# The squares of the even heads' rectified scores move from GpSimd to ScalarE, in a fused attention and mixture-of-experts kernel

## The chip, the cores and the metric

The kernel runs on one core of a Trainium2 chip. The metric is the device time of one execution in microseconds; runs of one kernel are compared by their medians. The profile is one further execution, taken by the hardware profiler.

## The reference

Sixteen batches of 256 tokens of width 128 pass through an attention layer with 16 heads (keys of 16, values of 64) and an expert layer (16 experts and a shared one). What matters here is the attention's non-linearity, which is no softmax:

```python
sim = jnp.einsum('bhid,bhjd->bhij', queries, keys)
attn = jnp.square(jax.nn.relu(sim))
aggr = jnp.einsum('bhij,bhjd->bhid', attn, values)
out = tanh_norm(aggr) * jnp.tanh(jax.nn.silu(gates))
```

Around it stand a layer norm, the projections of queries, keys, values and gates, the l2 norms of the heads, the output projection with its residual, a second layer norm, a router (group selection, top 4 of 16), the gate, up and down products of all experts, and a second residual.

## The kernel before

The kernel is a software pipeline written out by hand. A **step** s handles one batch in each of its stages at once: the layer norm and the query and key projections of batch s+2 ("L"), values and gates of batch s+1 ("P"), attention of batch s ("A"), output projection and second norm of batch s-1 ("O"), experts of batch s-2 ("F"). Steps run from -2 to 17, so attention is present in steps 0 to 15. Each step has eight **slots** k; in slot k attention handles the pair of heads 2k and 2k+1, and TensorE also does a list of other jobs, named in the table `FILL`. Every engine has its own program in the order of these slots, and semaphores tie them together.

In slot k TensorE does the fillers of the slot (L369 to L371 are the three-part products of the projections and experts, L422 a transpose, L428 a spread of per-row scales, L432 and L451 the output and down products, L437 the transpose of the second norm's rows), then the scores of the NEXT pair (`scores`, L478, into `ps_s`), then the products of THIS pair's squares with the values (L507, into `ps_a`). So between a pair's scores and their use lie the fillers of one slot.

ScalarE in slot k rectifies the pair's scores, one instruction for each head (L607, `ps_s` to `r`), squares the odd head (L610, `r` to `p`), then squares the previous pair's result for its norm (L619, `big<-ps_a`, called a2), then empties the slot's filler banks: queries and keys (L560, L562), values and their squares (L567, L570), gates (L576, and their tanh at L545), expert gates (L599), transposes (L586, L590, L591). GpSimd squares the even head in the same slot (L338, `r` times `r`), and has besides only two tiny roots a step (L330) and four scalings of the values (L354, slots 4 to 7). VectorE gates each pair's result (L904), sums the squares of the values (L748), takes the head norms by Newton steps (L662 to L670), runs the router (L800 to L843, ending in the expert weights `cs`, L794), and empties other banks (L741, L859, L867, L876, L883).

The filler banks are four, used in turn: a job may start when the job four places before it in the list has been read. This is how a late reader on ScalarE or VectorE holds up TensorE.

Of the kernel before, what the change touches and what calls it, by code (L numbers as in the profile page):

```python
# [8 lines left out]
ALU = mybir.AluOpType  # L9
# [12 lines left out]
def bass_attn_moe_layer_kernel(nc, tokens, Wqg, Wkv, Wout, gate_kernel, gate_bias,  # L22
# [45 lines left out]
    with ExitStack() as ctx:  # L68
# [3 lines left out]
        def sem(name):  # L72
            return ctx.enter_context(nc.semaphore(name))
# [101 lines left out]
        done = {k: sem(f"{k}_done") for k in JOBS}  # L175
        read = {k: sem(f"{k}_read") for k in JOBS}
        scores_done, values_done = sem("scores_done"), sem("values_done")
        relu_done, probs_even, probs_odd = sem("relu_done"), sem("probs_even"), sem("probs_odd")
        a2_done, aw_done = sem("a2_done"), sem("aw_done")
        ln1_ready, xh_ready, rstd1_ready, rstd2_ready = sem("ln1_ready"), sem("xh_ready"), sem("rstd1_ready"), sem("rstd2_ready")  # L180
        qk_squared = sem("qk_squared")
# [113 lines left out]
        @block.gpsimd  # L295
        def _(pool):
            n = [0]

            def built(ins):
                n[0] += 1  # L300
                ins.then_inc(consts_pool, 1)
                pool.wait_ge(consts_pool, n[0])


            built(pool.memset(minus_half[:], -0.5))
            built(pool.memset(ident[:], 0.0))
            built(pool.affine_select(out=ident[:], in_=ident[:], compare_op=ALU.not_equal, fill=1.0, base=0,
                                     pattern=[[-1, P]], channel_multiplier=1))
            built(pool.memset(selraw, 0.0))
            for part in range(2):  # L310
                view = selraw.rearrange("k c (e m) -> k c e m", e=2)
                built(pool.affine_select(out=view, in_=view, compare_op=ALU.not_equal, fill=1.0, base=-H * part,
                                         pattern=[[-2, NP], [-1, 2], [0, DV]], channel_multiplier=1))

            built(pool.memset(pick[:], 0.0))
            view = pick[:, 0:H].rearrange("p (a j e) -> p a j e", j=4, e=2)
            built(pool.affine_select(out=view, in_=view, compare_op=ALU.not_equal, fill=1.0, base=0,
                                     pattern=[[-2, 2], [-32, 4], [-1, 2]], channel_multiplier=1))
            view = pick[:, H:3 * H].rearrange("p (c j) -> p c j", j=8)
            built(pool.affine_select(out=view, in_=view, compare_op=ALU.not_equal, fill=1.0, base=-8,  # L320
                                     pattern=[[-32, 4], [-1, 8]], channel_multiplier=1))

            built(pool.memset(head16[:], 1.0))
            built(pool.affine_select(out=head16[:], in_=head16[:], compare_op=ALU.is_ge, fill=0.0, base=8 * DK,
                                     pattern=[[-DK, 32]], channel_multiplier=1))
            built(pool.affine_select(out=head16[:], in_=head16[:], compare_op=ALU.is_ge, fill=0.0, base=DK - 1 - 8 * DK,
                                     pattern=[[DK, 32]], channel_multiplier=-1))

            def root(dst, src, ready):
                pool.tensor_tensor(dst[:], src[:], minus_half[:].broadcast_to([P, T]), ALU.pow).then_inc(ready, 1)  # L330

            def step(s, q, on, at):
                for k in range(SLOTS):
                    if "A" in on:
                        h = 2 * k
                        wait(pool, values_done, 8 * s + k - 1)
                        pool.wait_ge(relu_done, 16 * s + h + 1)
                        pool.tensor_tensor(p[h % 4][:], r[0][:], r[0][:], ALU.mult).then_inc(probs_even, 1)  # L338
                    if k == 1 and "L" in on:
                        pool.wait_ge(ch_l, 3 * (s + 3))  # L340
                        root(rstd1, var1, rstd1_ready)
                    if k == 6 and "O" in on:
                        pool.wait_ge(ch_n, 3 * s)
                        root(rstd2, var2, rstd2_ready)
                    if "P" in on:
                        b = s + 1
                        if k in (4, 5, 6, 7):

                            t, half = divmod(k - 4, 2)
                            pool.wait_ge(vs_ready, b + 1)  # L350
                            pool.wait_ge(read["v"], 4 * b + k - 3)
                            view = v[1 - q][:, t, half * 512:(half + 1) * 512].rearrange("p (h d) -> p h d", d=DV)
                            scale = vs[:, t, half * NP:(half + 1) * NP]
                            pool.tensor_tensor(view, view, broadcast(scale, [P, NP, DV], 2), ALU.mult)\  # L354
                                .then_inc(v_normed, 1)

            run_steps(pool, step)


        @block.tensor  # L360
        def _(pe):
# [122 lines left out]
            def step(s, q, on, at):  # L484
                n = 0
                for k in range(SLOTS):
                    for stage, kind, j in FILL[k]:
                        if stage in on:
                            wait_for_bank(n, s, at)
                            filler(stage, kind, j, s, q, on, at)  # L490
                        n += 1

                    if k < SLOTS - 1:
                        if "A" in on:
                            scores(s, q, k + 1)
                    elif at is None or "A" in stages(at + 1):
                        scores(s + 1, 1 - q, 0)
                    if "A" in on:
                        wait(pe, aw_done, 8 * s + k - 1)
                        if k == 0:  # L500
                            pe.wait_ge(v_normed, 4 * s + 4)
                        for t in range(T):
                            for e in range(2):
                                h = 2 * k + e
                                if t == 0:
                                    pe.wait_ge((probs_even, probs_odd)[e], 8 * s + k + 1)
                                last = pe.matmul(ps_a[k % 2][64 * e:64 * e + 64, 0:N],  # L507
                                                 v[q][:, t, h * DV:(h + 1) * DV], p[h % 4][:, t * N:(t + 1) * N],
                                                 start=(t == 0), stop=(t == T - 1))
                        last.then_inc(values_done, 1)  # L510
# [5 lines left out]
        def _(act):  # L516
# [84 lines left out]
            def step(s, q, on, at):  # L601
                for k in range(SLOTS):
                    if "A" in on:
                        for h in (2 * k, 2 * k + 1):
                            wait(act, (probs_even, probs_odd)[h % 2], 8 * s + k)
                            act.wait_ge(scores_done, 16 * s + h + 1)
                            act.activation(r[h % 2][:], ps_s[h % 2][:], ACT.Relu).then_inc(relu_done, 1)  # L607
                        wait(act, values_done, 8 * s + k - 1)
                        act.wait_ge(relu_done, 16 * s + h + 1)
                        act.activation(p[h % 4][:], r[1][:], ACT.Square).then_inc(probs_odd, 1)  # L610

                    if ("A" in on and k > 0) or ("O" in on and k == 0):
                        pair, b = (k - 1, s) if k > 0 else (NP - 1, s - 1)
                        if pair == 0:
                            wait(act, done["ones"], s + 2)
                            if at == 0:
                                act.wait_ge(w_lo, 4)
                        act.wait_ge(values_done, 8 * b + pair + 1)
                        act.activation(a2[:, pair, :], ps_a[pair % 2][:, 0:N], ACT.Square).then_inc(a2_done, 1)  # L619
                    for stage, kind, j in FILL[k]:  # L620
                        if stage in on:
                            evacuate(stage, kind, j, s, q)
                        if (kind, j) == ("gu", 4) and "O" in on:
                            act.wait_ge(n_ready, s)
                            act.activation(nn[:], nn[:], ACT.Tanh).then_inc(tanh_n, 1)
                    for stage, kind, j in FILL[k - 1] if k > 0 else ():
                        if kind == "g" and stage in on and at != -1:
                            gates(j, s, q)
                    if at == 0 and k == 5:
                        expert_weights()  # L630
                if at == -1:

                    for j in range(4):
                        gates(j, s, q)
# [408 lines left out]
```

## Time and profile before

| what | us |
|---|---|
| median of 3 runs (797.83 to 801.03) | 798.34 |
| the profiled execution | 800.48 |
| its span, first to last instruction | 798.7 |
| busy: TensorE matmul | 686.5 (86%) |
| busy: TensorE weight loads (beside the matmuls) | 541.4 (68%) |
| busy: ScalarE | 502.6 (63%) |
| busy: VectorE | 485.6 (61%) |
| busy: GpSimd | 225.2 (28%) |

By the page's chain of the work that ended last, TensorE holds 53% of the span, VectorE 21%, ScalarE 12%. TensorE was granted 0.936 of its full clock on average. A busy share is an average over stretches that are bound by different engines, so it doesn't say by itself what an added instruction costs; for that the chain and the idle times have to be read place by place.

### The profile page before, as it was taken

Reading aid. Unit: us, or ns where it says so; the run is one execution under the profiler, and the core shown is the slowest. Engines: PE = TensorE matmul, PEld = TensorE weight load, DVE = VectorE, ACT = ScalarE, POOL = GpSimd, SP = SyncE. Lnnn points to the kernel's source line nnn. Section 1 sums busy time; section 2 is a strip of 40 time slices with the busy share of each in tenths; the row PEclk is TensorE's granted clock in tenths of the full one; section 3 lists DMA queues with packets and bytes.
Section 4 is the critical chain, followed back from the end, with each engine's and each line's share of the span. In section 5 each row is a group of like instructions: output and inputs, shape, how many; then the busy total and the mean of one; then the engine's idle time right before and its main releaser. Section 6 shows DMA issues by size and latency. Waiting matters only on the chain.

```text
span 798.7 us, 16206 instructions
## 1 busy us (share of the span) xinstructions
PE 686.5 (86%) x5160; PEld 541.4 (68%) x5160; DVE 485.6 (61%) x1739; ACT 502.6 (63%) x1114; POOL 225.2 (28%) x240
## 2 busy tenths in 40 slices
PE   1576798989989898999989898998989899989785
PEld 1454576858767686867767686876768686767675
DVE  3545657576565748576575757556584756655653
ACT  2387786676857666775766667585766667564311
POOL 2224331423223231422323242322323141331000
PEclk9878999999989999998999999899999899998898
DMA  8894869191734819093572909175471909200000
GB/s 201 133 149 54 127 99 108 25 143 25 130 50 83 91 60 118 7 137 41 99 78 70 101 31 133 21 118 60 88 83 53 118 0 139 35 14 2 7 8 7
DMA packets 72801, 60.83 MB, mean 76 GB/s; under 512 B 8624, under 2 KB 72496, under 8 KB 72752
## 3 DMA queue, kind: packets, MB, share of 16 engines
q1 hardware_dynamic: 72752, 60.26, 51.4%
q8 instruction: 21, 0.34, 0.2%
q14 instruction: 28, 0.23, 0.1%
HBM read 41.37 MB, written 18.87 MB: 75 GB/s over the span
## 4 chain that ended last, share of the span: by engine, by line
PE 53%; DVE 21%; ACT 12%; issue 8%; DMA 2%; POOL 1%; SPq 1%; ACTq 0%; DVEq 0%; POOLq 0%
PE ps_a L507 8%; PE ps_f L432 7%; PE ps_f L369 7%; PE ps_f L451 5%; PE ps_f L370 5%; PE ps_f L371 5%; PE ps_f L428 5%; PE ps_s L478 4%; ACT r L607 3%; PE ps_f L411 2%; DVE norms_m L748 2%; ACT sq L570 2%; DVE it L859 2%; DMA qkt<-qk_rows 2%; PE ps_f L422 2%
## 5 line engine op out<-in xcount | busy, mean ns | idle before, releaser
L338 POOL TENSOR_TENSOR p<-r 128x512 f32<-128x512 f32 x128 | 134.2, 1049 | 486.7 <-ACT r L607 484.4
L607 ACT ACTIVATE r<-ps_s 128x512 f32<-128x512 f32 x256 | 138.8, 598 | 66.1 <-PE ps_s L478 65.8
L507 PE MATMUL ps_a<-p,v 128*64 128x256 f32 x1024 | 139.5, 393 | 2.3 <-DVE big L904 1.3
L904 DVE TENSOR_TENSOR big<-ps_a,wt 128x256 f32<-128x256 f32 x128 | 53.8, 421 | 103.6 <-ACT big L619 103.6
L507 PEld LDWEIGHTS ps_a<-p,v 128*64 128x64 f32 x1024 | 62.8, 137 | 38.7 <-issue 2.9
L610 ACT ACTIVATE p<-r 128x512 f32<-128x512 f32 x128 | 80.9, 632 | 11.6
L859 DVE TENSOR_TENSOR it<-ps_f,it 128x256 f32<-128x256 f32 x144 | 59.0, 419 | 38.1 <-ACT it L599 37.0
L599 ACT ACTIVATE it<-ps_f 128x256 f32<-128x256 f32 x144 | 54.2, 391 | 34.1 <-PE ps_f L371 33.6
L451 PE MATMUL ps_f<-wdown,it 128*128 128x128 f32 x576 | 71.3, 280 | 2.9 <-DVE it L876 1.7
L451 PEld LDWEIGHTS ps_f<-wdown,it 128*128 128x128 f32 x576 | 68.5, 196 | 4.5 <-DVE it L876 1.8
L354 POOL TENSOR_TENSOR v<-v,vs 128x512 f32<-128x512 f32 x64 | 66.7, 1045 | 10.5 <-DVE vs L782 10.4
L478 PE MATMUL ps_s<-qkt 64*128 64x256 f32 x512 | 66.4, 337 | 2.7 <-DMA qkt<-qk_rows 2.6
L876 DVE TENSOR_TENSOR it<-ps_f,it 128x512 f32<-128x512 f32 x64 | 44.0, 689 | 37.8 <-PE ps_f L428 37.2
L432 PE MATMUL ps_f<-wout,big 128*128 128x128 f32 x512 | 62.4, 275 | 0.8 <-DVE big L867 0.8
L432 PEld LDWEIGHTS ps_f<-wout,big 128*128 128x128 f32 x512 | 59.7, 192 | 1.2 <-DVE big L867 1.2
L748 DVE TENSOR_REDUCE norms_m<-sq 128x8 f32<-128x512 f32 x64 | 43.7, 684 | 27.2 <-ACT sq L570 26.6
L422 PE MATMUL ps_f<-ident,cs 128*32 128x128 f32 x32 | 8.2, 351 | 58.6 <-DVE cs L794 58.6
L478 PEld LDWEIGHTS ps_s<-qkt 64*128 64x128 f32 x512 | 39.7, 191 | 25.3 <-issue 10.6
L576 ACT ACTIVATE wt<-ps_f 128x512 f32<-128x512 f32 x64 | 38.4, 601 | 27.6 <-PE ps_f L371 27.1
L619 ACT ACTIVATE big<-ps_a 128x256 f32<-128x256 f32 x128 | 47.1, 368 | 8.9 <-PE ps_f L411 8.6
L369 PE MATMUL ps_f<-x2h,weg_hi 128*128 128x256 f32 x144 | 49.7, 345 | 2.2 <-ACT sq L570 0.5
L867 DVE TENSOR_TENSOR big<-ps_f,big 128x512 f32<-128x512 f32 x64 | 41.0, 683 | 16.5 <-PE ps_f L428 16.4
(154 smaller groups left out, 1563.2 us busy)
## 6 DMA issues: line engine op xcount, KB each, us to landing
qk_rows<-qk_parts SPq DMA_DIRECT2D x16, 1024.0 KB, 4.4
qkt<-qk_rows SPq DMA_DIRECT2D x64, 256.0 KB, 9.5
qkt<-qk_rows SPq DMA_DIRECT2D x128, 128.0 KB, 9.0
x_in<-in_L_attn_tokens SPq DMA_DIRECT2D x16, 128.0 KB, 2.1
x_res<-in_L_attn_tokens SPq DMA_DIRECT2D x16, 128.0 KB, 14.2
out<-o_sb SPq DMA_DIRECT2D x16, 128.0 KB, 14.2
big<-in_L_attn_Wqg SPq DMA_DIRECT2D x1, 640.0 KB, 4.3
big<-in_L_attn_Wkv SPq DMA_DIRECT2D x1, 640.0 KB, 5.5
```

Of the source, the lines that this page charges most:

```text
L338: pool.tensor_tensor(p[h % 4][:], r[0][:], r[0][:], ALU.mult).then_inc(probs_even, 1)
L354: pool.tensor_tensor(view, view, broadcast(scale, [P, NP, DV], 2), ALU.mult)\
L369: pe.matmul(dst, stat[0], mov[0], start=True, stop=False)
L432: last = pe.matmul(ps[:, 0:D], aw[pb][:, c, tok[j]], wout[:, c, :], start=(c == 0), stop=(c == NP - 1))
L451: last = pe.matmul(ps[:, 0:D], it[:, c, tok[j]], wdown[:, c, :], start=(c == 0), stop=(c == FC - 1))
L478: last = pe.matmul(ps_s[e][:, t * N:(t + 1) * N], qkt[q][rows, 1, k, t * P:(t + 1) * P], qkt[q][rows, 0, k, :], start=True, stop=True)
L507: last = pe.matmul(ps_a[k % 2][64 * e:64 * e + 64, 0:N], v[q][:, t, h * DV:(h + 1) * DV], p[h % 4][:, t * N:(t + 1) * N], start=(t == 0), ...
L599: act.activation(it[:, j, :], ps[:, 0:N], ACT.Silu).then_inc(silu_done, 1)
L607: act.activation(r[h % 2][:], ps_s[h % 2][:], ACT.Relu).then_inc(relu_done, 1)
L610: act.activation(p[h % 4][:], r[1][:], ACT.Square).then_inc(probs_odd, 1)
L748: dve.tensor_reduce(ssv[:, t, half * NP:(half + 1) * NP], squares_at(j).rearrange("p (h d) -> p h d", d=DV), AX.X, ALU.add)\
L859: dve.tensor_tensor(it[:, c, :], bank[("gu", c)][:, N:2 * N], it[:, c, :], ALU.mult)\
```

## The change

GpSimd no longer squares the even heads. ScalarE does it: after the two rectifications of a pair come two squares, even head first. One semaphore (`probs_done`) now counts the squares of both heads, where two counted before. Nothing else is altered; buffers and their sizes stay.

```diff
@@ GpSimd
                 for k in range(SLOTS):
-                    if "A" in on:
-                        h = 2 * k
-                        wait(pool, values_done, 8 * s + k - 1)
-                        pool.wait_ge(relu_done, 16 * s + h + 1)
-                        pool.tensor_tensor(p[h % 4][:], r[0][:], r[0][:], ALU.mult).then_inc(probs_even, 1)
                     if k == 1 and "L" in on:
@@ TensorE
                                 if t == 0:
-                                    pe.wait_ge((probs_even, probs_odd)[e], 8 * s + k + 1)
+                                    pe.wait_ge(probs_done, 16 * s + h + 1)
@@ ScalarE
                         for h in (2 * k, 2 * k + 1):
-                            wait(act, (probs_even, probs_odd)[h % 2], 8 * s + k)
+                            wait(act, probs_done, 16 * s + h - 1)
                             act.wait_ge(scores_done, 16 * s + h + 1)
                             act.activation(r[h % 2][:], ps_s[h % 2][:], ACT.Relu).then_inc(relu_done, 1)
                         wait(act, values_done, 8 * s + k - 1)
-                        act.wait_ge(relu_done, 16 * s + h + 1)
-                        act.activation(p[h % 4][:], r[1][:], ACT.Square).then_inc(probs_odd, 1)
+                        for h in (2 * k, 2 * k + 1):
+                            act.wait_ge(relu_done, 16 * s + h + 1)
+                            act.activation(p[h % 4][:], r[h % 2][:], ACT.Square).then_inc(probs_done, 1)
```

The order of ScalarE's program in the first slot of a step inside the loop, before (L545 is the last tanh of the gates of the slot ahead, L607 the rectifications, L610 the odd square, L619 the a2 square):

```order
L545 ACTIVATE wt<-wt 128x512 [waits g_read]
L606 ISA [waits probs_even]
L607 ACTIVATE r<-ps_s 128x512 [waits scores_done]
L606 REGISTER_ALU [waits probs_odd]
L607 ACTIVATE r<-ps_s 128x512 [waits scores_done]
L211 REGISTER_ALU
L610 ACTIVATE p<-r 128x512 [waits relu_done,values_done]
L618 REGISTER_ALU
L619 ACTIVATE big<-ps_a 128x256 [waits values_done]
```

And with the change, where all line numbers are five or four lower:

```order
L540 ACTIVATE wt<-wt 128x512 [waits g_read]
L211 ISA
L601 REGISTER_ALU [waits probs_done]
L602 ACTIVATE r<-ps_s 128x512 [waits scores_done]
L601 REGISTER_ALU [waits probs_done]
L602 ACTIVATE r<-ps_s 128x512 [waits scores_done]
L211 REGISTER_ALU
L606 ACTIVATE p<-r 128x512 [waits relu_done,values_done]
L606 ACTIVATE p<-r 128x512 [waits relu_done]
L614 REGISTER_ALU
L615 ACTIVATE big<-ps_a 128x256 [waits values_done]
```

One 128x512 square has been added between the rectifications and everything that stands behind them in the slot. On GpSimd a step inside the loop, before, from its slot 4 to its end:

```order
L338 TENSOR_TENSOR p<-r 128x512 [waits relu_done]
L351 ISA [waits vs_ready]
L354 TENSOR_TENSOR v<-v,vs 128x512 [waits v_read]
L211 REGISTER_ALU
L337 REGISTER_ALU [waits values_done]
L338 TENSOR_TENSOR p<-r 128x512 [waits relu_done]
L351 REGISTER_ALU [waits vs_ready]
L354 TENSOR_TENSOR v<-v,vs 128x512 [waits v_read]
L211 REGISTER_ALU
L337 REGISTER_ALU [waits values_done]
L338 TENSOR_TENSOR p<-r 128x512 [waits relu_done]
L343 REGISTER_ALU
```

And with the change the whole of such a step (from L330 on in slot 1):

```order
L330 TENSOR_TENSOR rstd<-var,minus_half 128x2 [waits ch_l]
L346 ISA [waits vs_ready]
L349 TENSOR_TENSOR v<-v,vs 128x512 [waits v_read]
L346 REGISTER_ALU [waits vs_ready]
L349 TENSOR_TENSOR v<-v,vs 128x512 [waits v_read]
L338 REGISTER_ALU
L330 TENSOR_TENSOR rstd<-var,minus_half 128x2 [waits ch_n]
L346 REGISTER_ALU [waits vs_ready]
L349 TENSOR_TENSOR v<-v,vs 128x512 [waits v_read]
L346 REGISTER_ALU [waits vs_ready]
L349 TENSOR_TENSOR v<-v,vs 128x512 [waits v_read]
```

The scalings of the values (L354 before, L349 now) no longer stand behind a square of their slot; they wait for the scales alone, and the last two for the root of the second norm.

## Rows read from the trace of the kernel before

**Rows 1.** The page's groups: line engine op, shapes, count, busy, mean, idle before.
```profile
L338 POOL TENSOR_TENSOR p<-r 128x512 f32<-128x512 f32 x128 | 134.2, 1049 | 486.7 <-ACT r L607 484.4
...
L610 ACT ACTIVATE p<-r 128x512 f32<-128x512 f32 x128 | 80.9, 632 | 11.6
```
**Rows 2.** Chain of waits (start us, us, what): first relus of steps.
```profile
114.56 0.98 ACT r L607 x2
...
297.03 1.10 ACT r L607 x2
...
342.23 0.99 ACT r L607 x2
...
388.40 1.10 ACT r L607 x2
...
661.64 0.99 ACT r L607 x2
```
**Rows 3.** The same chain, last slot of the step that ends at 386.8 us.
```profile
383.95 0.09 ACT p L610
...
384.75 0.59 ACT qk_parts L560
...
385.86 0.04 DVE qk_parts L741
...
386.80 0.45 PE ps_f L437 x2
```
**Rows 4.** The same chain, first slot of the step that begins at 342.2 us.
```profile
344.62 0.57 ACT sq L570
...
345.23 0.39 PE ps_f L369
```
**Rows 5.** Waits, 160 to 680 us: who, for whom, total us, times, longest.
```profile
PE ps_f L422 <- DVE cs L794: 39.5, 11, 3.7
PEld ps_f L437 <- DVE o_sb L883: 3.6, 11, 0.4
```
**Rows 6.** Timeline of ScalarE: start us, us, instruction, count.
```profile
44.34 2.18 ACT L545 ACTIVATE wt<-wt 128x512 f32<-128x512 f32 x4
342.12 1.09 ACT L607 ACTIVATE r<-ps_s 128x512 f32<-128x512 f32 x2
343.30 0.63 ACT L610 ACTIVATE p<-r 128x512 f32<-128x512 f32 x1
343.84 0.37 ACT L619 ACTIVATE big<-ps_a 128x256 f32<-128x256 f32 x1
```
**Rows 7.** Waits of ScalarE from 160 to 680 us.
```profile
ACT r L607 <- PE ps_s L478: 46.8, 23, 2.8
ACT ct L586 <- PE ps_f L422: 20.4, 11, 1.9
ACT big L619 <- PE ps_f L411: 7.8, 12, 0.7
```
**Rows 8.** Timeline at 354 us; two lines by duration (ns, min/median/max).
```profile
353.53 1.04 POOL L338 TENSOR_TENSOR p<-r 128x512 f32<-128x512 f32 x1 [4.48 <-ACT r L607]
354.31 0.32 DVE L662 TENSOR_SCALAR norms_y<-norms_m 128x64 int32<-128x64 int32 x1
L662 DVE TENSOR_SCALAR norms_y<-norms_m x18: 195/319/968, 30.2 to 748.3; 128x64 int32<-128x64 int32 x18
L800 DVE SCALAR_TENSOR_TENSOR sc<-th,bias x16: 180/908/1025, 119.9 to 776.8; 128x32 f32<-128x32 f32 x16
```
**Rows 9.** Chain of waits at the start and near the end of the span.
```profile
56.25 0.98 DVE norms_y L662
...
94.40 0.94 issue
...
712.73 0.93 DVE norms_y L663
```
**Rows 10.** A stretch: length, busy by engine, granted clock, DMA share, GB/s.
```profile
360.00:362.00 2.00, 0.63 (x4) 0.59 (x5) 1.76 (x12) 0.15 (x1) 0.00 (x0) 0.55 1.15 111
```

More of the change, by code:

```diff
@@ L177, in bass_attn_moe_layer_kernel @@
         scores_done, values_done = sem("scores_done"), sem("values_done")
-        relu_done, probs_even, probs_odd = sem("relu_done"), sem("probs_even"), sem("probs_odd")
+        relu_done, probs_done = sem("relu_done"), sem("probs_done")
         a2_done, aw_done = sem("a2_done"), sem("aw_done")
```

## The prediction

> **What bounds the kernel now.** I read the page first, for the sizes: GpSimd's 128 squares and ScalarE's 128 [rows 1]. GpSimd is idle 72% of the span and ScalarE 37%, so neither is the bound as a whole; TensorE is busy 86% of it. Then I read the chain of waits, to see where a step's time is decided. Thirteen steps, 2 to 14, begin alike with two rectifications, the first of them at 114.56 and the last at 661.64 [rows 2]: (661.64 - 114.56) / 12 = 45.6 us a step. Within a step the chain has three parts.
>
> The first is the seam between two steps. In the last slot TensorE cannot start the transpose L437 before VectorE has read the query and key bank and the y2 bank; VectorE waits for ScalarE's two readings of that bank, and these stand behind the rectifications, the odd square and a2 [rows 3]. In the first slot of the next step it is the same again: rectifications, square, a2, the copy and the square of the values, and only then is the bank free in which TensorE's next expert product (L369, 345.23) goes [rows 4]. At both places TensorE already waits up to 0.4 us a step; the eleven rows of L437 show it for the seams between 160 and 680 us [rows 5]. So at both places ScalarE has no slack.
>
> The second part is VectorE's: sums of the squares, Newton steps, router, `cs`. TensorE stands idle 39.5 / 11 = 3.6 us a step until `cs` is there [rows 5]. The third is slots 3 to 7, some 21 us in which TensorE never waits and ScalarE does: its waits for scores, for the transposed weights and for the ones product are in [rows 7].
>
> **The change part by part.** (a) One square more on ScalarE, in each of 128 pairs. It lasts 0.632 us [rows 1], but instructions of this engine overlap when nothing holds them apart. Two rectifications take 1.09 us, and one takes 0.60, so the second starts 0.49 after the first; a square and the next instruction start 343.84 - 343.30 = 0.54 apart; four tanh of 512 columns from and to SBUF start (2.18 - 0.63) / 3 = 0.52 apart [rows 6]. In the kernel before the odd square starts at 343.30, which is 0.69 after the second rectification (342.12 + 0.49 = 342.61): 0.2 us are a wait for that rectification's end. With the change the even square fits into this wait, since its own input is long there: even square at 342.61 + 0.49, odd square 0.53 later, next instruction 0.54 after that, at 344.17 where it was 343.84. The added time is 0.33 us a pair. I take that. Its bounds: not below 0.3, since the odd square can't be started sooner; at most 0.63, if the even square, too, starts only 0.69 after the rectifications or the two squares don't overlap. The row shows 0.54 between a square and the next start. The Trainium skill (ScalarE: Activation LUTs, section What ACT_TABLE_LOAD costs) says that back-to-back instructions overlap by about 93 ns only; by its overlap the square would add 632 - 93 = 0.54 us, an estimate that speaks against the change and agrees with the row as to one square alone, but leaves out the wait of 0.2 us that is now filled; the sum would be (0.54 - 0.33) x 27 = 5.7 us higher.
>
> (b) Where does it count? At the seam both times: last slots of steps 2 to 13, twelve, and first slots of steps 2 to 14, thirteen. 25 x 0.33 = +8.3 us. In the last two slots of step 1 the chain also goes over ScalarE: 2 x 0.33 = +0.7.
>
> (c) Where it is hidden. Slot 1: a2 waits 7.8 / 12 = 0.65 us for the ones product, twice what is added. Slot 2: VectorE is busy with its own chain till after the expert gates are there. Slot 3: the emptying of the transposed weights waits 20.4 / 11 = 1.9 us for TensorE. Slots 5 to 7: the scores come 46.8 / 23 = 2.0 us after ScalarE is ready [rows 7]. In slot 4 the waits for TensorE are smaller, but nobody waits for what stands there. If this cover were gone, each slot would cost 0.33 us more.
>
> (d) What GpSimd gives back. Some VectorE instructions stand still while a GpSimd square runs. The square from 353.53 ends at 354.57, and L662, started at 354.31, ends just behind it at 354.63: 0.32 us, where its least is 0.195. L800, 32 columns, takes 0.908 us in the median and 0.18 when no square runs [rows 8]. L662 is on the chain in each of the 13 steps: 13 x (0.319 - 0.195) = -1.6 us. L800 is not: behind it VectorE waits for a2 and again for the values' square, which TensorE sets, so its 0.73 us go into idle time. Late next is a2. By the Trainium skill (SBUF - State Buffer, section Who interferes with whom) an instruction of VectorE with two SBUF inputs, or in a two-port mode, is blocked for the whole of a GpSimd instruction that reads SBUF; these two rows agree.
>
> (e) The first two steps. ScalarE is nearly full there and leads the chain through about ten pairs, which comes to 10 x 0.33 = +3.3 us. On the other side five VectorE instructions of the chain are held up by GpSimd, the first at 56.25 (0.98 instead of 0.20), the last at 94.40 (0.94 of waiting), each worth about 0.75: -3.8. I book 0 for both together, with an uncertainty of 2 us either way. Near the end L663 at 712.73 loses 0.93 - 0.20 us in the same way: -0.7 [rows 9].
>
> (f) GpSimd's own later work. The scalings of the values now run as soon as the scales are there, in slot 3 and 4 and in slot 6, earlier than before. The products that use them come in the next step: nothing. The last of them may hold up VectorE's normed rows in slot 6, which TensorE uses only behind the seam's other waits: nothing. If that cover went, one such hold costs at most the length of a GpSimd instruction, 1.05 us [rows 1], a step. The odd and even squares are ready 0.35 us later than the later of them was; TensorE uses them one slot on, about 2 us after: nothing.
>
> The sum is 8.3 + 0.7 - 1.6 - 0.7 + 0 = +6.7 us on the profiled 800.48. That execution stood 2.1 us over the median; I carry the difference to the median: 798.34 + 6.7 = **805.0 us**, 0.8% slower.
>
> **TensorE's clock.** After the wait for `cs` the granted clock falls, 0.55 in the stretch 360 to 362 [rows 10], that is to the lower level of 1.2 GHz for part of it, and steps differ: 342.23 - 297.03 = 45.2 us for one, 388.40 - 342.23 = 46.2 for the next [rows 2], the longer one with the longer time at the low level. Which steps get the longer one can shift with the step's length. The chain's rows of the thirteen steps show about one long step in three, so four of twelve; if none were long it would give 4 us, if six were it would cost 2. This is in the range.
>
> **The rivals.**
> R1, hidden: ScalarE's added time vanishes even at the seam, because the transpose and the product there are set by something else (VectorE's order, TensorE's own work ahead of them). For it: TensorE's waits there are small, 3.6 / 11 = 0.33 us. Against it: the chain goes over ScalarE without a gap. Then 0.7 - 1.6 - 0.7 = -1.6: about 797.
> R2, faster: the relief of VectorE reaches the chain. L800's 0.73 us come off the path to `cs`, beside L662's 0.12, and the added squares are hidden as in R1: 13 x 0.85 + 0.7 + 3.8 = -15.5 against +3.3 in the first steps, so -12: about 786. It decides from the point where VectorE has no idle time between L800 and the sums. Against it: L800 is followed by idle time on VectorE before a2 and before the sums.
> R3, the squares don't overlap: 0.63 us a pair. The seam costs 25 x 0.30 = 7.5 more, the last two slots of step 1 0.6, the start up to 3: about 815.
> R4, the clock falls at the seam too. TensorE's waits there double. If each of the twelve steps lost as much as a long step loses against a short one, 1.0 us, the time would be about 817. For it: idle time is what preceded the low clock at `cs`. Against it: that idle time was 3.6 us in one piece, and this is about 0.7 twice.
> That the change doesn't do what it says can be left aside: the order shows the added square in every slot.
>
> **How the numbers follow.** Forecast 0.62, R1 0.17, R2 0.05, R3 0.10, R4 0.06. A measurement of this kernel can tell about 0.5%, 4 us, from no change: faster is below 794.3, slower above 802.3. The forecast's own range is 805 with -4 and +2 for the clock and 2 either way for the start, so 800 to 809; a fifth of its chance, 0.12, lies below 802.3. Slower: 0.50 of the forecast, R3 and R4, together 0.66. Same: 0.12 of the forecast and 0.14 of R1, together 0.26. Faster: R2 and the 0.03 of R1 in which the clock gives too, together 0.08. The range goes from R1's time, 797, to short of R3's full price, 813.
>
> **What would show it.** Right: the second square starts 0.53 us after the first, and a2 1.56 us after the second rectification where it was 1.23; TensorE's wait before L437 is about 0.65 us a step instead of 0.33, and before the first slot's L369 likewise; L662 takes 0.195 us and L800 0.18; the step is 46.1 us on average. R1 would show the step unchanged at 45.6; R2 a shorter wait for `cs`; R3 0.63 us at a pair; R4 a granted clock below 1.00 around the seam. The forecast is wrong if the step changes by less than 0.2 or more than 1.0 us.

## The result and the profile after

The changed kernel takes 843.91 us (median of 4 runs, 840.92 to 848.17) against 799.57 us before in the same comparison: the ratio is 1.056, 95% interval 1.0505 to 1.0614. It is slower, as forecast, but by 44 us, where 6.7 were forecast with a range up to 813. The profiled execution took 842.76 us, its span is 840.9.

The page's groups for the lines of [rows 1], line and engine first, then count, busy time and mean, and the idle time ahead with its releaser:

```profile
L602 ACT ACTIVATE r<-ps_s 128x512 f32<-128x512 f32 x256 | 139.5, 601 | 89.7 <-PE ps_s L473 59.0
...
L606 ACT ACTIVATE p<-r 128x512 f32<-128x512 f32 x256 | 148.6, 642 | 0.0
```

There are 256 squares now where there were 128, at 0.642 us, and GpSimd's are gone. That is what was planned. What is new is the idle time ahead of the rectifications: it is 89.7 us, and only 59.0 of it is a wait for scores. ScalarE's waits between 160 and 720 us name most of the rest (engine and line, releaser, total us, times, longest):

```profile
ACT r L602 <- PE ps_s L473: 41.1, 26, 2.4
ACT r L602 <- issue: 30.6, 8, 4.3
```

Eight times ScalarE stood for about 4 us ahead of a rectification and waited for nothing that the profile shows. The kernel before has no such row among ScalarE's waits. TensorE's waits over the same stretch show who pays:

```profile
PE ps_f L417 <- DVE cs L790: 38.1, 11, 3.5
PE ps_f L364 <- ACT sq L565: 36.2, 12, 8.7
```

and its weight loads over the same stretch:

```profile
PEld ps_f L432 <- DVE o_sb L879: 7.8, 12, 0.7
```

The wait for `cs` is as it was in [rows 5]. The wait of the first slot's L364 for the values' square is 36.2 us in place of nearly nothing, up to 8.7 us at once. The chain of waits shows one of these places (start us, us, what; "issue" is time without a visible cause, ACTq is ScalarE's sequencer; L197 is the step of the loop's counter and its jump):

```profile
299.40 0.52 ACT wt L540
299.92 3.65 issue
303.56 0.06 ACTq L197
...
303.74 0.06 ACT r L602
303.80 4.81 issue
308.62 0.05 ACT r L602
```

The two stops stand at the jump back of ScalarE's loop: one of 3.65 us right behind the jump, then four instructions of the loop's body, then one of 4.81, in whose first 0.6 us the rectification ahead of it still runs. The loop runs over steps 4 to 13, two steps in one pass, so it jumps back four times, 4 x 2 = 8 stops. The lengths of the steps say the same. From its slot 0 in step 0 to that in step 5 the changed kernel needs 206.5 us against 205.0 before, which is near the forecast. From step 5 to step 13, with the four jumps, it needs 407.2, that is 50.9 a step, against 45.4 before.

TensorE pays twice. At this jump it stands 8.7 us waiting for the values' square, and in the stretch behind its granted clock is at half, 0.50. Such a stretch of 7 to 10 us follows each of the four jumps. The first one, and the same place in a kernel with the same work but without stops (a_pad16, below), as views of a stretch (length, busy time of PE, PEld, DVE, ACT and POOL, granted clock, DMA share, GB/s):

```profile
308.00:317.00 9.00, 5.45 (x30) 3.22 (x34) 4.01 (x16) 6.71 (x15) 0.69 (x1) 0.50 1.16 130
```

```profile
300.00:317.00 17.00, 15.82 (x128) 11.33 (x124) 11.42 (x47) 14.66 (x36) 0.69 (x1) 1.00 1.03 144
```

Where no stop is, ScalarE does what part (a) of the prediction said. The first slot of step 7, to be held against [rows 6] (start us, us, line, instruction, count):

```profile
356.65 1.08 ACT L602 ACTIVATE r<-ps_s 128x512 f32<-128x512 f32 x2
357.61 1.17 ACT L606 ACTIVATE p<-r 128x512 f32<-128x512 f32 x2
358.65 0.40 ACT L615 ACTIVATE big<-ps_a 128x256 f32<-128x256 f32 x1
```

The second rectification starts at 356.65 + 1.08 - 0.60 = 357.13, the first square 0.48 later, the second 1.17 - 0.63 = 0.54 behind it, a2 at 358.65. That is 1.52 us behind the second rectification where it was 1.23 and 1.56 were forecast: the added time is 0.3 us a pair. So it is in seven of the eight slots (medians 1.20 to 1.25 before, 1.51 or 1.52 now); in slot 1, where a2 waits for the ones product, it is 1.98 and 2.06. And the VectorE lines of [rows 8], by duration (ns, min/median/max), are free of GpSimd:

```profile
L658 DVE TENSOR_SCALAR norms_y<-norms_m x18: 195/195/197, 30.7 to 792.4; 128x64 int32<-128x64 int32 x18
L796 DVE SCALAR_TENSOR_TENSOR sc<-th,bias x16: 181/182/183, 121.7 to 820.6; 128x32 f32<-128x32 f32 x16
```

### The profile page after: what moved, and what is told of

Same layout as the page of the kernel before. It is cut to its first block, busy times and chain, and to the rows that moved or that the text cites. A ratio compares the mean times of both kernels' runs of the same rounds, so it can differ in the third digit from the quotient of the medians.

```text
span 840.9 us, 16075 instructions
## 1 busy us (share of the span) xinstructions
PE 692.2 (82%) x5160; PEld 541.7 (64%) x5160; DVE 473.0 (56%) x1739; ACT 552.7 (66%) x1242; POOL 92.1 (11%) x112
## 4 chain that ended last, share of the span: by engine, by line
PE 51%; DVE 19%; ACT 13%; issue 12%; DMA 2%; POOL 1%; SPq 1%; ACTq 0%; DVEq 0%; POOLq 0%
PE ps_a L502 9%; PE ps_f L427 7%; PE ps_f L364 7%; PE ps_f L366 5%; PE ps_f L446 5%; PE ps_f L365 5%; PE ps_s L473 4%; PE ps_f L423 4%; ACT p L606 3%; PE ps_f L406 2%; DVE norms_m L744 2%; ACT sq L565 2%; DMA qkt<-qk_rows 2%; DVE it L855 2%; PE ps_f L417 2%
## 5 line engine op out<-in xcount | busy, mean ns | idle before, releaser
L602 ACT ACTIVATE r<-ps_s 128x512 f32<-128x512 f32 x256 | 139.5, 601 | 89.7 <-PE ps_s L473 59.0
L606 ACT ACTIVATE p<-r 128x512 f32<-128x512 f32 x256 | 148.6, 642 | 0.0
L502 PE MATMUL ps_a<-p,v 128*64 128x256 f32 x1024 | 144.7, 400 | 0.1
L349 POOL TENSOR_TENSOR v<-v,vs 128x512 f32<-128x512 f32 x64 | 65.3, 1043 | 282.4 <-DVE vs L778 282.4
L502 PEld LDWEIGHTS ps_a<-p,v 128*64 128x64 f32 x1024 | 64.6, 139 | 38.8 <-issue 3.7
L364 PE MATMUL ps_f<-x2h,weg_hi 128*128 128x256 f32 x144 | 50.3, 349 | 37.7 <-ACT sq L565 37.0
L594 ACT ACTIVATE it<-ps_f 128x256 f32<-128x256 f32 x144 | 55.9, 403 | 29.6 <-PE ps_f L366 29.0
L330 POOL TENSOR_TENSOR rstd<-var,minus_half 128x2 f32<-128x2 f32 x32 | 22.1, 690 | 437.7 <-DVE var L678 437.7
L364 PEld LDWEIGHTS ps_f<-x2h,weg_hi 128*128 128x128 f32 x144 | 31.4, 218 | 49.0 <-ACT sq L565 44.6
L615 ACT ACTIVATE big<-ps_a 128x256 f32<-128x256 f32 x128 | 50.3, 393 | 9.8 <-PE ps_f L406 9.5
```

The source lines that it names most:

```text
L364: pe.matmul(dst, stat[0], mov[0], start=True, stop=False)
L502: last = pe.matmul(ps_a[k % 2][64 * e:64 * e + 64, 0:N], v[q][:, t, h * DV:(h + 1) * DV], p[h % 4][:, t * N:(t + 1) * N], start=(t == 0), ...
L594: act.activation(it[:, j, :], ps[:, 0:N], ACT.Silu).then_inc(silu_done, 1)
L606: act.activation(p[h % 4][:], r[h % 2][:], ACT.Square).then_inc(probs_done, 1)
```

## Experiments: what stops ScalarE at the jump

The page's list of DMA queues (packets, MB, share of the 16 engines) has two that carry instructions. Queue q8 has 21 packets in both kernels. Queue q14, after and before:

```profile
q14 instruction: 47, 0.39, 0.2%
```

```profile
q14 instruction: 28, 0.23, 0.1%
```

So the suspicion was code. The packets of q14 are of 8192 bytes, and their times in the trace bear it out. At the first jump of the changed kernel, at 298.9 us, one packet arrives at 302.37 and one at 307.16, 1.2 and 1.5 us ahead of the ends of the two stops. At the three other jumps, too, a packet arrives 1.2 to 1.7 us ahead of each stop's end. In the kernel before, whose first jump is at 296.1, no packet of q14 travels between 285.3 and 327.9 us, and ScalarE's sequencer goes on 0.2 us behind the jump. (Behind the third jump one packet travels in every kernel with a loop, with stops or without.) In the trace's count ScalarE's loop begins at its instruction 409 before and 441 after, and its body has 267 and 282 instructions. The 32 more ahead of the loop are one a slot in the four steps ahead of it. **Theory A**: the body must lie on few enough blocks of fetched code; the stop behind four instructions of the body says that a border lies there, at 445. **Theory B**: the stops come from the work itself or the length of the body.

The pad kernels add nothing but waits that are long satisfied, two to an instruction, where ScalarE idles at the start (a_pad130 has 70 of its 130 later, in step -1):

```diff
             act.wait_ge(consts_pool, 3)
+            for _ in range(2 * PAD):
+                act.wait_ge(consts_pool, 3)
```

**b_pad32**: the kernel before with 32 of them.

> The kernel before, its squares untouched, with 32 more instructions on ScalarE ahead of its loop: waits that are long satisfied, put where ScalarE idles at the start. They move the loop's first instruction by as much as the change did (409 to 441 in the trace's count). Theory A (the loop of the changed kernel begins four instructions ahead of a border between blocks of fetched code, so that its body lies on one block more than ScalarE holds, and each jump back waits for code): stalls of some 3.7 and 4 us at four jumps, 799.6 + 4 x 8.5 = about 834 us (825 to 840). Theory B (the changed kernel's stalls come from what it does, the second square and its longer body of 282 instructions): no stall, 799 to 802 us.

It took 841.84 us (839.51 to 843.44), ratio 1.0511 (1.0483 to 1.054). Without any change of the work, 32 instructions of padding bring back the whole loss. That is 2 us over the range expected, which priced the stops alone and not the clock behind them. Its waits of ScalarE between 290 and 690 us have the row of the changed kernel:

```profile
ACT r L609 <- issue: 30.7, 8, 4.5
```

**b_pad48**:

> The kernel before with 48 such instructions in place of 32. Theory A: the loop now begins 12 instructions behind the border, its 267 instructions lie on no more blocks than they did, no stall, 800 us (798 to 802); this run also prices the padding. If any shift, or the padding itself, costs time: 830 or more, as with 32.

799.51 us, ratio 0.9984 (0.9968 to 1.0). Padding as such costs nothing.

**a_pad16**: the changed kernel with 16.

> The changed kernel with 16 such instructions ahead of ScalarE's loop; the computation is the same. Theory A: the loop begins 12 instructions behind the border, no stall at a jump, and what is left is the price of the change itself, which the prediction put at +6.7 us: 806 us (802 to 812). Theory B (the body of 282 is too long wherever it lies): 844 us as before.

803.74 us (798.22 to 805.49), ratio 1.0035 (1.0006 to 1.0064). Theory B is out: the long body runs without a stop. So 843.9 - 803.7 = 40 us of the loss are the stops at jumps with what follows from them, and the work of the change costs 3.6. The waits of TensorE for L364 between 160 and 720 us are 36.2 us in the changed kernel; in a_pad16 they are 4.7 (160 to 680 us). The rest fits the lower clock behind the stops: the mean granted clock is 0.925 over 840.9 us against 0.934 over 803.8, so by an estimate 0.075 x 840.9 - 0.066 x 803.8 = 10 us more of the full clock are withheld.

**a_pad130**: the changed kernel with 130.

> The changed kernel with 130 such instructions, 60 at the start and 70 in slot 5 of step -1, where ScalarE idles 5 us. The loop then begins 126 instructions behind the border. If blocks are of 256 instructions and two are held, as the Trainium skill has it (Runtime: NRT & Kernel Launch, section Instruction fetch mechanics), 126 + 282 = 408 is less than 512: no stall, 806 to 810 us. If blocks are of 128 instructions (the profile's fetches are of 8192 bytes) and three are held, 126 + 282 = 408 is more than 384: the stall is back, 835 to 845 us.

849.96 us, ratio 1.0628 (1.0603 to 1.0653). The stops are back, at a time 5 us over the expected range; why it is 6 us slower than the changed kernel is not shown. Its chain of waits at the first jump:

```profile
299.36 0.52 ACT wt L542
299.88 3.66 issue
303.54 0.06 ACTq L197
...
303.64 0.04 ACTq L606
303.68 4.01 issue
307.68 0.06 ACT r L607
```

The second stop comes sooner in the body: two instructions are ahead of it here, four in the changed kernel. That puts borders at 441 + 4 = 445 and 571 + 2 = 573, 128 apart. **Theory A3** says so: blocks of 128 instructions, three held at once. One packet of 8192 bytes would be one block if an instruction takes 64 bytes.

**a_pad3 and a_pad4** differ by one instruction.

> The changed kernel with 3 long satisfied waits more ahead of ScalarE's loop. Theory A3 (blocks of 128 instructions, three held; a border 4 instructions behind the changed kernel's loop start): the loop now begins on the last instruction ahead of the border, 127 + 282 = 409, over 384: stalls as in the changed kernel, 842 to 850 us. If the border is elsewhere: 804.

> The changed kernel with 4 in place of 3. Theory A3: the loop begins exactly on the border, 0 + 282, no stall: 804 us (800 to 807). A cause that has to do with the amount of work or of instructions can't tell 3 from 4: both alike.

a_pad3: 847.52 us (ratio 1.0585, 1.0554 to 1.0616). a_pad4: 803.37 us (1.0021, 0.9987 to 1.0056). One padding instruction more ahead of the loop is worth 44 us. In a_pad3 the second stop stands behind a single instruction of the body, and 444 + 1 = 445: the third kernel that puts the border there or 128 behind.

All kernels with a loop on ScalarE together, with the loop's start counted from the last border (at 445, or by the distance of 128 at 317) and the body added:

| kernel | loop starts at | behind a border | + body | us |
|---|---|---|---|---|
| before | 409 | 92 | 359 | 799.6 |
| mix (below) | 402 | 85 | 347 | 789.6 |
| seam (below) | 394 | 77 | 364 | 794.0 |
| b_pad48 | 457 | 12 | 279 | 799.5 |
| a_pad4 | 445 | 0 | 282 | 803.4 |
| a_pad16 | 457 | 12 | 294 | 803.7 |
| a_still (below) | 457 | 12 | 298 | 808.9 |
| ends (below) | 453 | 8 | 308 | 809.3 |
| inner (below) | 453 | 8 | 315 | 798.5 |
| b_pad32 | 441 | 124 | 391 | 841.8 |
| after | 441 | 124 | 406 | 843.9 |
| a_pad130 | 571 | 126 | 408 | 850.0 |
| a_pad3 | 444 | 127 | 409 | 847.5 |

Up to 364 there is no stop, from 391 on there are two at each jump. The page counts 47 or 48 packets on q14 in the last four kernels and 27 to 29 in the others. Three blocks of 128 instructions, 384, fit both sides; that the limit is 384, and nothing else between 364 and 391, no run shows. The Trainium skill (Runtime: NRT & Kernel Launch, section Instruction fetch mechanics) says that a taken branch whose target is not among the blocks that are held forces a fetch before execution goes on, and these runs agree; it gives blocks of 256 instructions, two held, and there the runs differ, since a_pad130 would have fitted and the second stop puts a border at 573. The other kernels of the table would come out alike with blocks of 256, two held, and a border at 445.

**a_flat** takes the jump away altogether, with ScalarE's steps written out one behind the other:

```diff
-            run_steps(act, step)
+            run_flat(step)
```

> The changed kernel with ScalarE's program written out flat, without a loop (1786 instructions in place of 442 + 282 + 226), order of work unchanged. Theory A: without a jump back nothing is fetched late, 804 us (800 to 808), as with the aligned loop. If code can't be fetched ahead at ScalarE's pace even in a straight line: over 810.

791.11 us (786.72 to 792.41), ratio 0.9895 (0.9868 to 0.9922). No stop, as theory A has it. But it is 12 us faster than the aligned loop with the same work, and 9 us below the expected range. That had to be explained before the change could be priced.

## Experiments: the clock at the wait for cs

In every wait for `cs` TensorE idles 3.5 us, in a_flat as in the aligned loop. Before, the granted clock falls to half behind that wait [rows 10]. In a_flat it does not. The wait's end and the stretch around it in step 7 of a_flat, the TensorE row of the timeline and two stretches:

```profile
362.38 0.38 PE L417 MATMUL ps_f<-ident,cs 128*32 128x128 f32 x2 [3.47 <-DVE cs L790]
```

```profile
360.00:362.00 2.00, 0.00 (x0) 0.00 (x0) 1.65 (x14) 1.46 (x4) 0.00 (x0) 1.00 1.17 115
362.00:364.00 2.00, 1.62 (x14) 1.64 (x15) 1.90 (x11) 0.76 (x2) 0.00 (x0) 1.00 1.14 114
```

TensorE is idle for the whole of the first stretch, and the clock stays at 1.00, its upper level of 2.4 GHz. In a_flat's profiled execution, the fastest of five (786.72 us), each of the steps 6 to 13 takes 44.38 or 44.39 us, and no wait of them costs clock. The aligned loop's steps take 45.57 and 46.58 in turn. Theory C: whether such a wait costs clock hangs on where in time the waits fall, and so on the length of the step; 44.39 happens to repeat a lucky place. Theory D: flat code is faster by itself.

> The kernel before with ScalarE's program written out flat. a_flat came out at 791.1 where the aligned loop takes 803.7, with the granted clock at 1.00 in every step from the sixth on, though TensorE waits for cs as long as before. Theory C (whether a wait for cs costs clock hangs on the length of the step; a_flat's step of 44.39 us happens to keep it): the work of before has another step length, 45.2 and 46.2, and keeps it: 800 us (797 to 802). Theory D (a program without loop registers and jumps is faster by itself): 788 us (785 to 791).

> a_flat with one 128x32 copy more on ScalarE behind the squares of slot 0, into a tile nobody reads: about 0.15 to 0.25 us a step at the seam. Theory C: the step leaves the length at which no wait costs clock, the falls are back in most steps, and the time goes to 804 or so (798 to 808), far more than the copies take. Theory D: 16 x 0.2 = +3, 794 us (793 to 796).

b_flat, the kernel before with flat code on ScalarE: 802.49 us, ratio 1.0036 (1.0023 to 1.0048), not faster, and half a microsecond over theory C's range. a_flat_nudge adds to a_flat one tiny copy a step:

```diff
+                        if k == 0:
+                            act.activation(scratch[:], ident[:, 0:32], ACT.Copy)
```

804.59 us (803.5 to 807.77), ratio 1.0066 (1.0043 to 1.0088). Some 0.2 us of work in each of 16 steps costs 13.5 us. Its steps are 45.7 to 46.8 us again, and the clock falls in each: the stretch behind its wait for `cs`, which ends at 366.7 us in the step that answers to the one above:

```profile
366.00:368.00 2.00, 1.33 (x7) 1.30 (x8) 1.83 (x11) 0.37 (x1) 0.00 (x0) 0.50 1.16 114
```

Theory D falls. Theory C foretold what happened; which places in time are lucky, and why, no run here shows. The price of the change's work is then read where the clock falls once in each step, as before: +3.6 us for a_pad16 in the medians, and a kernel's luck with the clock can be worth 12 us, three times that.

## Experiments: the terms of the sum

These kernels but a_still come from one table that says for each slot which engine squares the even and the odd head, with a semaphore for each engine. The table below is that of mix, P for GpSimd and A for ScalarE, and the edit is shortened and set against the kernel before:

```diff
+        OWN = [('P', 'P'), ('P', 'A'), ('A', 'A'), ('A', 'A'), ('P', 'A'), ('P', 'A'), ('P', 'A'), ('P', 'P')]
-                        act.wait_ge(relu_done, 16 * s + h + 1)
-                        act.activation(p[h % 4][:], r[1][:], ACT.Square).then_inc(probs_odd, 1)
+                        for h in (2 * k, 2 * k + 1):
+                            if OWN[k][h % 2] == "A":
+                                act.wait_ge(relu_done, 16 * s + h + 1)
+                                act.activation(p[h % 4][:], r[h % 2][:], ACT.Square).then_inc(probs["A"], 1)
```

**ends** moves the even squares in slots 0 and 7 alone (with the padding that its loop needs), **inner** in slots 1 to 6 alone.

> One part of the change alone: the even squares go to ScalarE in slots 0 and 7, and stay with GpSimd in slots 1 to 6; the loop is aligned by 36 instructions (8 + 300 = 308). My term (b): 25 x 0.33 = +8, and 0.7 in step 1: 808 us (804 to 811), more than the whole aligned change (803.7), since nothing is given back at L662. If the cost is spread over all slots: 801.

> The other part alone: even squares on ScalarE in slots 1 to 6, on GpSimd in slots 0 and 7; aligned by 20 instructions (8 + 307 = 315). My term (c), hidden, with (d) given back: 800 - 1.6 - 0.7 and up to -1 in the first steps: 797 us (794 to 799). If the added square costs in every slot: 805 or more.

ends: 809.32 us, ratio 1.0113 (1.0091 to 1.0134). inner: 798.48 us, 0.9976 (0.9964 to 0.9989). Both within 1.5 us of what was expected. Two slots carry the whole cost of the work, the six others carry none and even give a little back, 1 to 3 us by the interval.

**a_still** is a_pad16 with GpSimd squaring on, into a tile that nobody reads; ScalarE waits for `spare_done` before it overwrites `r[0]`.

```diff
+                    if "A" in on:
+                        h = 2 * k
+                        pool.wait_ge(relu_done, 16 * s + h + 1)
+                        pool.tensor_tensor(scratch[:], r[0][:], r[0][:], ALU.mult).then_inc(spare_done, 1)
```

> The changed kernel, loop aligned by 16 instructions as in a_pad16 (803.7 us), but GpSimd goes on squaring the even heads, into a tile that nobody reads; ScalarE's rectification waits for it before it writes over its input. It prices what GpSimd gives back. My terms (d) and (e): 1.6 + 0.7 at L662 and L663 and up to 3.8 in the first steps, so 804 + 6 = 810 us (807 to 812). If VectorE's stalls beside GpSimd are off the path: 804.

808.92 us, ratio 1.01 (1.0084 to 1.0116), 5.2 us over a_pad16 where 6 were expected. TensorE's waits at the seam are as in a_pad16. The line of [rows 8] is slow again in it:

```profile
L668 DVE TENSOR_SCALAR norms_y<-norms_m x18: 194/315/1081, 30.8 to 760.6; 128x64 int32<-128x64 int32 x18
```

**seam** turns the change round: in slots 0 and 7 GpSimd does both squares.

> The other way round, from the kernel before: in slots 0 and 7 GpSimd takes both squares and ScalarE none, in the other slots all is as before. Its ScalarE loop lies on three blocks (77 + 287 = 364, under 384), so no stall at a jump. My theory that ScalarE has no slack at the seam: a2 and what follows it come 0.7 us earlier there, of which TensorE can use what it waits today, 0.33 at L437 and about as much at the first slot's L369: 25 x 0.33 = -8 us, 792 us (789 to 796). If ScalarE isn't what ends TensorE's waits at the seam: 800. If GpSimd's second square comes too late for TensorE: over 802.

794.03 us, ratio 0.9922 (0.9909 to 0.9936): ScalarE was what TensorE waited for at the seam, in the kernel before too. GpSimd's two squares, one row of its timeline in slot 7, are done at 382.04, 1.6 us after the rectifications and before TensorE's use at 384.19 by that kernel's chain:

```profile
380.00 2.04 POOL L350 TENSOR_TENSOR p<-r 128x512 f32<-128x512 f32 x2 [2.24 <-ACT r L619]
```

**mix** puts the findings together: both squares on GpSimd in slots 0 and 7, both on ScalarE in 2 and 3, one each in the rest.

> What the terms together suggest: both squares on GpSimd in slots 0 and 7 (ScalarE has no slack there), both on ScalarE in slots 2 and 3 (slack there, and GpSimd's square holds up L662 and, in the first steps, L670, L668 and L793), the others as before. Loop on three blocks (85 + 262 = 347). -8 for the seam, -1.6 -0.7 for L662 and L663, up to -3 in the first steps: 788 us (785 to 793). If the seam gives nothing: 796.

789.6 us, ratio 0.9855 (0.9824 to 0.9887), 1.5% faster than the kernel before. Between 160 and 680 us TensorE's matmul row has one wait in mix, that for `cs`. In a_pad16 it also has 5.5 us at L432 and 4.7 us at L364, the two places of the seam; the kernel before has 0.2 us there:

```profile
PE ps_f L434 <- DVE cs L809: 41.6, 12, 3.5
```

**mix_flat** is mix with flat code on ScalarE.

> mix (789.6 us) with ScalarE's program flat. Theory C: its step of 44.8 us with one fall of the clock stays as it is, 789 us (785 to 791). Theory D: 789.6 - 12 = 778 us.

788.27 us, ratio 0.9859 (0.9839 to 0.9879), the same as mix, as theory C has it. Both beat both kernels of this study by more than 10 us.

## Why the prediction was wrong

**What failed** is the sum: it has no term for the added instructions as code, and the text gives no reason for that. The parts (a) to (f) count what the added instructions cost on the engines and in the waits. None counts what they are as code: 32 instructions more ahead of ScalarE's loop and 15 more in it, net, which put its body on one block more than is held. The runs showed in its place two stops of ScalarE at each of the loop's four jumps back, which cost 40 of the 44 us; the 32 instructions ahead of the loop are enough for it by themselves (b_pad32). The loop's length and place could be counted in the trace of before, and its page listed queues that carry code; where the borders lie and how many blocks are held came only from the runs. Code was not among the rivals either, and R3 and R4, which were, reach only 815 and 817. So the forecast had the direction right by luck: what made the kernel clearly slower is not what it named.

**Part (a)**, 0.33 us a pair on ScalarE: 0.29 by the timeline. Right, and so was the ground: the even square fills a wait that was there. By the overlap that the Trainium skill gives (ScalarE: Activation LUTs, section What ACT_TABLE_LOAD costs) the sum would have been 5.7 higher. Two squares in a row do start 0.54 apart, as that section and [rows 6] have it, but a_pad16 is not dearer than forecast. R3, which had 0.63 us a pair, is out.

**Part (b)**, all cost at the seam: right. ends shows it alone (+9.1 us, forecast 9.0 with the two slots of step 1), seam shows the other sign. TensorE's wait before L432 is 7.8 / 12 = 0.65 us, as forecast, in the changed kernel and in a_pad16. The wait for the values' square, at L369 before and at L364 in a_pad16, grows as well; the rows of the weight loads between 160 and 680 us, before and a_pad16:

```profile
PEld ps_f L369 <- ACT sq L570: 8.1, 24, 0.4
```

```profile
PEld ps_f L364 <- ACT sq L567: 11.4, 23, 0.6
PEld ps_f L432 <- DVE o_sb L881: 7.8, 12, 0.7
```

R1, the hidden cost, is out by this. In a_pad16 the steps 2 to 13 take 6.0 us more than before, where 12 x 0.5 were forecast; in ends they take 4.2 us more with one fall of the clock fewer, so the agreement of its total to 0.1 us is in part luck.

**Part (c)**, the rest hidden: right, by inner.

**Parts (d) and (e)**, what GpSimd gives back: 5.2 us by a_still, where 1.6 + 0.7 + 3.8 = 6.1 were expected. The total is near, its split is not. The two profiled executions are 7.2 us apart: 2.6 of it lie ahead of step 2 (forecast 3.8), 0.4 in steps 2 to 13 (forecast 1.5) and 4.0 behind the loop's last steps, from step 15 on (forecast 0.7). There a_still has two long falls of the clock where a_pad16 has two short ones, so the end was mis-sized. L662's part shows in TensorE's wait for `cs`, 39.3 / 11 = 3.57 us in a_still against 38.1 / 11 = 3.46 in a_pad16, but hardly in the length of the steps. R2, which had 0.85 us a step come off that wait, is out.

**The clock**: that the fall behind the wait for `cs` varies with the step's length was seen, how much it can be worth was not. The text allowed for -4 and +2 us. The runs show -12 for a_flat, and a_flat_nudge gives it back. In the aligned kernel, with its 45.57 and 46.58 in turn, each second step pays the dearer fall where each third did. In a_pad16 no fall stands at the seam, so R4 is out.

**The sum**, +6.7 us: a_pad16 measures +3.6 (0.5 to 5.1 by its interval) and has its mean step at 46.08 us, where 46.1 were forecast. The 3 us between lie from step 15 on, where that execution has two short falls of the clock in place of two long ones; a_still, with GpSimd's squares back, has the long ones again. So without the stops the forecast's range would have held, but the slowdown would have been 0.35% (0.06 to 0.64) where 0.8% was forecast, less than the 0.5% that the prediction called the least to be told.

## What to carry to other kernels

When an edit adds instructions to an engine that runs a loop, count them as code: where the loop begins, how long its body is, and on how many blocks it lies, which were of 128 instructions here; a body on three blocks ran freely, one on four paid two stops of about 4 us at every jump, and one padding instruction decided it. Once TensorE stood for them, its clock fell too. Test it by padding before the work is blamed. And price work by the place where it stands: the same 0.3 us cost nothing in six slots and everything in two, which also says where a slower but idle engine should take it over.

## What the runs showed of the hardware

Three things were unexpected. ScalarE's stops behind a taken jump: 3.6 to 3.8 us right behind the jump, then 2.0 to 5.2 us more at the next border (sixteen jumps in four kernels), whenever start and body came to 391 instructions or more from a border, with a packet of 8192 bytes of instructions arriving 1.0 to 1.7 us ahead of each stop's end. The granted clock at a 3.5 us idle stretch of TensorE: it fell in the kernel before [rows 10] and stayed at 1.00 from step 6 to step 14 of a_flat's profiled execution, whose steps took 44.38 us. And the dependency of the square on its rectification leaves ScalarE a gap that an independent square fills, so that the second square of a pair cost 0.29 us where two squares in a row start 0.54 apart.
